# Graph attention on one core: three of four block transposes move behind the last maxima of their group

## The reference

```
q, k, v = heads(x @ Wq + bq), heads(x @ Wk + bk), heads(x @ Wv + bv)
scores  = q @ k^T / sqrt(32) + beta * adj        # per head, 256 x 256
scores  = where(adj > 0, scores, -9e15)
out     = softmax(scores) @ v                    # heads side by side again
result  = layernorm(x + out)
```

## Time and profile before

| | us |
|---|---|
| median of 3 runs | 679.05 (678.77 to 679.55) |
| the profiled execution | 678.75 |
| its span, first to last instruction | 677.0 |
| TensorE busy | 635.4 (94%) |
| VectorE busy | 597.7 (88%) |
| ScalarE busy | 576.0 (85%) |
| GpSimd busy | 406.9 (60%) |
| mean granted TensorE clock | 0.993 of full |

### The profile page before, as it was taken

How to read it: one execution, slowest core, us unless ns; L and a number is a source line. 1 busy time by engine, 2 the same in 40 slices (tenths; PEclk the granted TensorE clock), 3 DMA queues, 4 the chain that set the end, 5 groups by cost and what they waited for, 6 DMA issues and landing times. The chain is left out here.

```text
span 677.0 us, 21340 instructions
## 1 busy us (share of the span) xinstructions
PE 635.4 (94%) x6304; PEld 514.5 (76%) x6304; DVE 597.7 (88%) x2385; ACT 576.0 (85%) x2024; POOL 406.9 (60%) x642
## 2 busy tenths in 40 slices
PE   5899999999999999999999999999999999999981
PEld 5788877787878787878777777888787878787850
DVE  3898899988999898989898989898989998898974
ACT  4799888889898889898888888888989888988881
POOL 3413266766566775566775556676556676566743
PEclk9999999999999999999999999999999999999997
DMA  8065556567656557755557755556765556765441
GB/s 254 4 148 142 139 136 166 126 164 187 172 143 162 137 140 189 185 150 153 145 122 187 187 155 151 153 119 177 188 172 144 154 127 157 189 168 144 114 101 70
DMA packets 68226, 101.93 MB, mean 151 GB/s; under 512 B 10512, under 2 KB 36368, under 8 KB 68112
## 3 DMA queue, kind: packets, MB, share of 16 engines
q1 hardware_dynamic: 67024, 100.37, 57.9%
q10 hardware_dynamic: 1088, 0.20, 0.2%
HBM read 22.94 MB, written 12.58 MB: 52 GB/s over the span
## 5 line engine op out<-in xcount | busy, mean ns | idle before, releaser
L433 ACT ACTIVATE probs<-neg_scores,neg_max 128x256 f32<-128x256 f32 x768 | 382.4, 504 | 4.4 <-DVE neg_max L515 2.9
L515 DVE CUSTOM_DVE_ANT_0 neg_scores<-s_bank,bias_sb 128x256 f32<-128x256 f32 x768 | 282.3, 416 | 54.2 <-ACT probs L433 45.0
L554 DVE STREAM_TRANSPOSE blocks<-probs 128x512 f32<-128x512 f32 x248 | 171.3, 700 | 0.0
L433 ACT ACTIVATION_READ_ACCUMULATOR probs<-neg_scores,neg_max 128x1 f32 x768 | 149.8, 195 | 0.0
L326 PE MATMUL j_bank<-xt_high,w_high 128*128 128x256 f32 x576 | 115.6, 309 | 1.9 <-ACT w_high L465 1.5
L399 PE MATMUL s_bank<-qk 32*128 32x256 f32 x1536 | 110.0, 399 | 5.4 <-DVE neg_max L515 3.7
L399 PEld LDWEIGHTS s_bank<-qk 32*128 32x128 f32 x1536 | 72.6, 184 | 46.7 <-ACT v_sb L452 28.1
L760 POOL TENSOR_SCALAR o_sb<-y_sb,rstd,shift 128x384 f32<-128x384 f32 x60 | 99.3, 1662 | 9.6 <-POOL shift L755 9.6
L326 PE MATMUL j_bank<-xt_high,w_low 128*128 128x256 f32 x576 | 99.5, 280 | 0.0
L326 PE MATMUL j_bank<-xt_low,w_high 128*128 128x256 f32 x576 | 99.2, 280 | 0.0
L369 PE MATMUL j_bank<-ident,probs 128*128 128x128 f32 x544 | 84.1, 278 | 13.9 <-issue 12.8
(11 more groups left out here) (56 smaller groups left out, 899.2 us busy)
## 6 DMA issues: line engine op xcount, KB each, us to landing
shuffled<-blocks SPq DMA_DIRECT2D x496, 128.0 KB, 3.1
x_sb<-in_x_dram SPq DMA_DIRECT2D x32, 384.0 KB, 3.3
out_dram<-o_sb SPq DMA_DIRECT2D x30, 384.0 KB, 4.3
adj_sb<-in_adj_dram SPq DMA_DIRECT2D x32, 256.0 KB, 3.7
out_dram<-o_sb SPq DMA_DIRECT2D x4, 192.0 KB, 2.1
blocks<-in_L_gnn_Wq_dram SPq DMA_DIRECT2D x1, 576.0 KB, 5.8
blocks<-in_L_gnn_Wk_dram SPq DMA_DIRECT2D x1, 576.0 KB, 8.2
blocks<-in_L_gnn_Wv_dram SPq DMA_DIRECT2D x1, 576.0 KB, 9.6
```

Of the source, the lines that this page charges most:

```text
L433: nc.scalar.activation(probs[:, (T * s + t) % (T * NX), :], neg_scores[:, (T * s + t) % (T * NH), :], ACT.Exp, bias=neg_max[:, n % 2, t, h ...
L515: nc.vector.tensor_tensor_reduce(neg_scores[:, (T * s + t) % (T * NH), :], s_bank[h % J][:, t * N:(t + 1) * N], bias_sb[:, n % 2, t, :], - ...
L554: nc.vector.transpose(blocks[:, n % 2, :, h, :, :].rearrange("p k t q -> p t k q"), probs[:, slot:slot + T, :].rearrange("p t (k q) -> p t ...
```

## The change

VectorE's loop turned each head's blocks in that head's step of the loop. Now it turns a group's first head as before, and the second, third and fourth together in the fourth head's step, behind the maxima issued there. Nothing else differs.

```diff
                     if h % J in (2, 3) and s + 4 < B * H:
                         maxima(s + 4)
-                    if by_blocks(n, h):
-                        turn_blocks(n, h)
+
+                    if h % J in (0, 3):
+                        for head in (h,) if h % J == 0 else range(h - 2, h + 1):
+                            if by_blocks(n, head):
+                                turn_blocks(n, head)
                     if h == 0 and n + 1 < B:
                         edges(n + 1)
```

## The result

The changed kernel takes 675.9 us (675.41 to 676.22, 6 runs) against 679.3 us (678.77 to 680.0, 6 runs). The ratio is 0.9949, with a 95% interval of 0.9936 to 0.9961: faster by 3.4 us. Forecast were 2.2 us and 676.9. Two executions on record ran at a mean granted clock of 0.56 and 0.75 (1027.11 us of the kernel before, 778.57 of the first run under "The next link of the loop") and are left out of every comparison.

What follows compares the result with a forecast made beforehand. A batch loop through VectorE's maxima and TensorE's second scores was taken as the bound. 27 batches x 0.05 = 1.35, plus 0.32, plus 0.5, is 2.2 us, so 676.9; range 675.0 to 679.3.

Steps and rivals of the forecast that it cites:

- the larger gain: Rival: the whole 0.09 us at the second scores lands in each batch, 3.6 us in all, 675.4; chance 0.12.
- The bound: Second scores wait about 0.09 us for VectorE's maxima on the batch loop; third scores coming earlier is worth nothing.
- The rival that took 1.09 us for TensorE's own length: No change at head sums to second scores, the 0.15 us a coincidence; only 0.8 us gained, 678.2; chance 0.22.
- (a): Heads 4 to 7: last maxima end 1.26 us earlier, second scores stop waiting; head 8's maxima gain 0.05 us a batch.
- the two long batches: Two batches losing more at the second scores, near 327.54 and 550; gain capped by VectorE's idle 0.16 each, 0.32 us.
- (b): Before head 8's maxima VectorE does four transposes, same sum within 0.02 us, free at 309.71 with 0.10 left as cover.
- (c): Heads 8 to 11, same edit: VectorE's stretch from 309.87 to 319.14 keeps its length; worth nothing.
- (d): ScalarE's exponentials of head 7 need head 1's slot, with 1.3 us to spare; no new wait, worth nothing.
- (f): Batch 0 and the start: VectorE's idle times fill with transposes, ScalarE must come earlier too; 0.5 us, ends 0 and 0.9.
- Transposes that don't overlap: Rival: each VectorE transpose in a row takes 0.70 us rather than 0.60; slower, 688 us; chance 0.08.

Runs made afterwards that it cites:

- the first run under "The next link of the loop": Changed kernel with the third X and K jobs moved between the next batch's maxima of heads 0 and 1 in step h = 9: 656.95 us, ratio 0.9668.
- The experiments on either side: Against the changed kernel, heads 1 to 3 turned ahead of head 7's maxima: 696.79 us; separately, heads 5 to 7 ahead of head 11's: 678.98 us.

## Why the prediction was right, point by point

The direction, what bounds the kernel and the range held. The size held only roughly: 3.4 us lies outside the band of 1.4 to 3.0 that the prediction called its forecast (0.52) and next to the 3.6 of the larger gain (0.12).

- **The bound.** That the second scores wait for the maxima although no idle time shows, and that what the third scores wait costs nothing, held. The experiments on either side (18.1 us and 0.0 for the same delay) show it. The rival that took 1.09 us for TensorE's own length fell with 1.00 in each of the batches 2 to 29.
- **(a) the wait.** Taken as 0.05 us in 27 batches plus 0.32 for two, 1.67 in all. Measured, from head 4's maxima to head 8's, 0.068 a batch, 1.9 over 28: 0.21 and 0.26 in the two long batches, where 0.16 each was taken, and 0.055 in each of the others. The held and unheld steps (2.40 and 2.34 us from head sums to maxima) were the right rows to price it; the larger 0.09 is what the scores gained, not the maxima behind them.
- **(b), (c) the queue.** "The same within 0.02" was the right bound, but not nothing: 0.019 us a batch in the second group, 0.56 us in the run with that group alone. The working misread the pair in the kernel before. It took both for 0.70 us long and 0.60 apart; the second one, by itself, is

```profile
308.96 0.67 DVE L554 STREAM_TRANSPOSE blocks<-probs 128x512 f32<-128x512 f32 x1
```

  so it starts 0.63 behind the first (308.33) and is itself the shorter one, with its successor 0.59 behind (309.56). The steps were 0.63, 0.63, 0.63 and 0.59 and are now 0.63 and three of 0.59: 0.07 less, not 0.06, and the sum held all the same.
- **(d) new waits.** None, with 1.4 us to spare.
- **(f) the start.** This term was mis-sized: 0.5 us, with 0.9 as its upper end, measured 1.14. The upper end was TensorE's idle time before the third scores of batch 0. The longest wait (the 1.4 in the earlier trace rows) stands one group before, at the second scores, and was not counted; and ScalarE, which was to cap the gain, was itself idle behind these held scores, for the matmuls that follow them. The kernel before, TensorE and then ScalarE:

```profile
30.14 1.15 PE L399 MATMUL s_bank<-qk 32*128 32x256 f32 x16 [1.43 <-DVE neg_max L515]
...
31.69 0.39 ACT L454 ACTIVATE xt_high<-j_bank 128x256 fp32r<-128x256 f32 x1 [0.49 <-PE j_bank L335]
...
33.81 0.48 ACT L450 ACTIVATE qk<-j_bank,qk_bias 128x256 f32<-128x256 f32 x1 [0.73 <-PE j_bank L326]
```

  In the changed kernel the same scores wait 0.22 us and ScalarE 0.18 in the same stretch. Counted from the first scores at all, the second scores of batch 0 come 1.24 us earlier, the third 1.55, and the high part that was to be the cap 1.06 (38.72 before, 38.32 after). The trace after shows VectorE's steps in batch 0:

```profile
29.33 2.49 DVE L554 STREAM_TRANSPOSE blocks<-probs 128x512 f32<-128x512 f32 x4
...
31.82 0.38 DVE L515 CUSTOM_DVE_ANT_0 neg_scores<-s_bank,bias_sb 128x256 f32<-128x256 f32 x1
...
37.48 0.38 DVE L515 CUSTOM_DVE_ANT_0 neg_scores<-s_bank,bias_sb 128x256 f32<-128x256 f32 x1
...
38.81 0.43 DVE L536 TENSOR_TENSOR xt_low<-j_bank,xt_high 128x256 fp32r<-128x256 f32 x1
```

  From the maxima at 31.82 to those at 37.48 it is 5.66 us (31.46 to 37.69 before, 6.23), from there to the low part 1.33 (39.13 before, 1.44). The maxima at 31.82 were 0.30 earlier already, so this makes 0.98 of the 1.14; the rest comes in batch 1. More goes than the idle time of 0.42: without it the second of these maxima starts 0.30 us behind the first, not 0.35.
- **The rivals.** Transposes that don't overlap would have been 0.70 a step; in rows of two, three and four they measured 0.63 behind the first and 0.59 behind the others. The Trainium skill (VectorE: DVE Perf Modes, The DRAIN you can't avoid) states that the next operation doesn't start until the pipeline is empty, which is all that the prediction cited; the same section adds that a next operation that is not held starts earlier. This trace is in line with the addition: each transpose starts 0.07 to 0.08 us before the row of the one in front of it ends. The larger gain came out by its number (3.6 forecast, 3.4 measured), but not by its mechanism: it wanted 0.09 us in every batch, and it was 0.068 plus 0.019 and a start that gave twice what I took.

The sum missed by 1.2 us of 3.4: 0.6 at the start, 0.5 in transposes in a row, 0.2 in the wait, less 0.1 in the rest of the batch.

## What to carry to other kernels

Where one engine's starts keep the same distance behind another engine's last result while its own spacing varies, it is being held, even if its busy row shows no gap; compare the spacing with a place where the same pair is free. Then find the loop: price a delay at each hand-over, as one of 0.68 us cost 18 us at one group's scores and nothing at the next, whose slack of 0.67 it just used up. Once a wait is gone, moving more is worth nothing; the next link (here two instructions behind the wrong maxima, 19 us) is worth more than the rest of the first.

## What the runs showed of the hardware

- A semaphore's way from VectorE's read-out of the maximum to TensorE's first score matmul took 0.15 us wherever the scores were held, in batches of every kernel here (62 places in the kernel before); from VectorE's low part to TensorE's turn it was 0.10, in the 28 batches of the kernel before that show the wait.
- A block transpose of 128 x 512 behind another kind of instruction is 0.70 us long and has its successor 0.63 behind it; one that follows a transpose is 0.67 long, with its successor 0.59 behind. This holds whatever the successor is, in all 248 of the kernel before and of the changed one.
- After 1.86 us without a matmul in batch 0, TensorE's granted clock was 0.57 over the next 4 us (a mean between its two levels, 1.2 and 2.4 GHz) and 1.00 again after that. After 2.01 us, in the kernel with heads 1 to 3 in front, it was 0.50 from 32.2 to 35.5. In the kernel before, whose longest hole there is 1.43, and in the changed kernel it was 1.00 throughout this stretch, in the executions traced.
